# A two-layer block on one core: ascending chunk order, operands of the first heads loaded chunk by chunk, routing moved among the first row maxima

## The chip, the cores and the metric

One core of a Trainium2 chip. Five engines run their own instruction streams side by side: TensorE (PE, with its weight loads as PEld), VectorE (DVE), ScalarE (ACT), GpSimd (POOL) and SyncE (SP), which here only issues DMAs. The metric is the time of one execution on the device in microseconds (us); lower is better.

## The reference

2048 tokens of 256 features go through two gated layers, each `x = x + s * silu(g)` with `xn = layernorm(x)` in front.

```python
# layer 0: s = linear attention by running sums, g = ternary-weight projection
q, k = elu(q) + 1, elu(k) + 1
out = q * cumsum(k * v) / (q * cumsum(k) + 1e-9)
# layer 1: s = causal softmax attention, 16 heads of 16, with a position slope per head
scores = where(causal, q @ k.T / 4 + slope[h] * (k_pos - q_pos), -1e9)
s = softmax(scores) @ v @ out_w.T + out_b
# g = mixture of 8 experts, the best 2 of each token
logits = xn @ gate_w.T + gate_b
routing = softmax(top_k(logits, 2))
for e in range(8):
    h = xn @ w1[e].T + b1[e]
    y = h[:, 0::2] * sigmoid(1.702 * h[:, 0::2]) * (h[:, 1::2] + 1)
    g += (y @ w2[e].T + b2[e]) * routing_weight[:, e]
```

## The kernel before

Layer 0 takes the first 150 us. Then come the projections of layer 1, in four **chunks** of 512 tokens (`c`, `NC = 4`). For each chunk PE makes four 128x512 blocks `m` of q and k. ACT evicts each into `QV` and rounds it to bf16 (`QP[.., 0]`), DVE subtracts (L1032, into `QR`), ACT rounds the rest (L728), DVE subtracts again (L1041); the three bf16 parts go by DMA into the DRAM tensor `qk_parts` (SP, L357). A head's operands in `OPS` are loaded from there by `load(h)`: 6 DMAs of 16 to 48 rows, each over all 2048 columns (L369). On top of them 12 rows with positions and slopes are needed: for heads 0 to 3 ACT writes them (`first_of`, L766), for later heads POOL (`rows`, L527, four instructions for two heads).

Attention runs over 8 **pairs** of heads. A pair has four chunks of queries, taken in `ORDER = (0, 3, 1, 2)`; chunk `a` has 8(a+1) score tiles of up to 128x512, so a pair has 80 tiles and the whole 640. All engines walk through the same numbered **steps** `n`. In step `n`

- PE makes A tile `n` (`score_a`, L1424, masked by L1427) and DVE reduces it to row maxima (`reduce_a`, L1163);
- PE makes B tile `n - 44` (`score_b`, L1444; `LEAD = 44`), the same scores less their row maximum, ACT takes the exponential (L811), and every fourth step PE multiplies four of them with the values (L1466).

Between the two passes, each chunk `m` (numbered through the pairs, four to a pair) needs a **turn**: when its last A tile is reduced, DVE writes `NM` (L1171), POOL splits it in five small instructions into three bf16 parts `NP` (`maxima(m)`, L540 to L548), PE transposes `NP` (`turn_maxima`, L1474) at step `TURN_AT`, ACT copies it to `MT` (L793), and SP writes it by DMA as three more rows of `OPS`, for which the chunk's first B tile waits. `turn_maxima` waits for the five instructions of POOL; everything behind it on PE waits with it.

POOL's order in pair `p` (1 to 6) is fixed in the code:

```python
maxima(NC * p)
maxima(NC * p + 1)
pool.wait_ge(b_scored, PER_PAIR * p)      # the pair before has made its last B tile: step 80p + 43
rows(2 * p + 2); rows(2 * p + 3)          # four instructions of 12x2048
head_values(2 * p + 2); head_values(2 * p + 3)
maxima(NC * p + 2)
maxima(NC * p + 3)
```

The expert layer runs among the same steps. DVE finds the two best experts of each token and each token's place in its expert's list: first some 50 small instructions by themselves (L1081 to L1110), then 15 in steps 3 to 17 (`slots`). ACT and POOL split the normalized tokens in two f16 parts (`XR`, L773 and L560), POOL scatters the rows by 32 indirect DMAs (L569) between `maxima(0)` and `maxima(3)`. 23 blocks of 256 rows follow, block `b` at step `84 + 20b` (24 matmuls of L1361 over eight steps, the 8 of L1371 14 steps later: `down`). In the last pair (`p = 7`) POOL gathers the results by 32 indirect DMAs (L580) between its `maxima`, and DVE adds them up (`add_experts`). Bank 7 is shared by turns, `heads_out` (L1481) and `down`, each of which waits until the one before has been read out.

Of the kernel before, what the change touches and what calls it, by code (L numbers as in the profile page):

```python
# [14 lines left out]
ALU = mybir.AluOpType  # L15
# [3 lines left out]
P = 128  # L19
# [19 lines left out]
ORDER = (0, 3, 1, 2)  # L39
# [12 lines left out]
FIRST_BLOCK, EVERY = 84, 20  # L52
# [30 lines left out]
TURN_AT = {chunk_end(m) - 1 + (3, 4, 5, 3)[m % NC]: m for m in range(NC * PAIRS)}  # L83
HEADS_AT = {chunk_end(m) - 1 + LEAD + (15, 11, 11, 11)[m % NC]: m for m in range(NC * PAIRS)}
# [5 lines left out]
END_PAIRS = [2 * c + r for c in ORDER for r in range(2)]  # L90
END_AT = {650: 0, 655: 1, 661: 2, 665: 3, 675: 4, 679: 5}
# [11 lines left out]
def build(nc, x, w_qkv0, w_out0, w_ffn, b_ffn, w_qkv1, b_qk1, b_v1, w_out1, b_out1, slopes, pos_rows, pick,  # L103
          masks, ident, sel, table, gate_w, gate_b, w1, b1, w2, b2, out):
    ctx = ExitStack()
    with ctx:
# [3 lines left out]
        def sem(name):  # L110
# [39 lines left out]
        TH = sb("TH", [P, 2, CH])  # L150
        GT = sb("GT", [P, 2, CH])
# [32 lines left out]
        XTH, XTL = XT[:, 0], XT[:, 1]  # L184
        WQG = 3 * D + E
# [11 lines left out]
        TAB = pr32[:, S + D:S + D + E * NT + 8 + 24]  # L197
# [27 lines left out]
        QV = ops32[:, 0:2048].rearrange("p (m n) -> p m n", m=4)  # L225
        QR = ops32[:, 2048:4096].rearrange("p (m n) -> p m n", m=4)
        QP = ops32[:, 4096:7168].bitcast(BF16).rearrange("p (m j n) -> p m j n", m=4, j=3)
# [33 lines left out]
        v_copied, lg_copied, gsplit, route = (  # L261
            sem("v_copied"), sem("lg_copied"), sem("gsplit"), sem("route"))
        expd, rstep, ones_rows, we_done, wet_ps = (
            sem("expd"), sem("rstep"), sem("ones_rows"), sem("we_done"), sem("wet_ps"))
# [12 lines left out]
        hot, count_ps, chain, slots_done, xr_high, xr_low = (  # L277
            sem("hot"), sem("count_ps"), sem("chain"), sem("slots_done"), sem("xr_high"), sem("xr_low"))
# [10 lines left out]
        b2_zero, wet_zero = sem("b2_zero"), sem("wet_zero")  # L289
# [31 lines left out]
        def _(sp):  # L321
# [31 lines left out]
            with sp.Fori(0, NC) as c:  # L353
                for m in range(4):
                    side, half = m // 2, m % 2
                    sp.wait_ge(qk_p2, 4 * c + m + 1)
                    sp.dma_start(parts[side, :, half * P:half * P + P, ds(c * CH, CH)].rearrange("j f t -> f j t"),  # L357
                                 QP[:, m, :, :]).then_inc(parts_out[m], 16)

# [1264 lines left out]
```

## Time and profile before

| | |
|---|---|
| time, median of 3 (lowest to highest) | 972.3 us (968.9 to 974.0) |
| the profiled execution's own time | 969.48 us |
| its span | 967.7 us, of mean granted TensorE clock 0.923 |
| PE busy | 796.4 us (82%) |
| DVE busy | 635.3 us (66%) |
| ACT busy | 498.7 us (52%) |
| POOL busy | 313.9 us (32%) |

Busy time is a share of the whole span. A PE that shows busy is not at its peak, since matmuls are pipelined. The row of the page with the span in 40 slices of 24.2 us each shows where PE is not busy: up to slice 5 (layer 0), in slices 8 and 9, and in slice 33:

```
PE   4474659914889999999999999999999995888986
```

### The profile page before, as it was taken

Reading aid. Unit: us, or ns where it says so; the run is one execution under the profiler, and the core shown is the slowest. Engines: PE = TensorE matmul, PEld = TensorE weight load, DVE = VectorE, ACT = ScalarE, POOL = GpSimd, SP = SyncE. Lnnn points to the kernel's source line nnn. Section 1 sums busy time; section 2 is a strip of 40 time slices with the busy share of each in tenths; the row PEclk is TensorE's granted clock in tenths of the full one; section 3 lists DMA queues with packets and bytes.
Section 4 is the critical chain, followed back from the end, with each engine's and each line's share of the span. In section 5 each row is a group of like instructions: output and inputs, shape, how many; then the busy total and the mean of one; then the engine's idle time right before and its main releaser. Section 6 shows DMA issues by size and latency. Waiting matters only on the chain.

```text
span 967.7 us, 13783 instructions
## 1 busy us (share of the span) xinstructions
PE 796.4 (82%) x4910; PEld 387.1 (40%) x4910; DVE 635.3 (66%) x1197; ACT 498.7 (52%) x1030; POOL 313.9 (32%) x363
## 2 busy tenths in 40 slices
PE   4474659914889999999999999999999995888986
PEld 1242345403324444444544444444444432222543
DVE  5999997665856666676566667666666763984121
ACT  2343315861555565555555655555565552556340
POOL 2766963121660060051006005100600516340111
PEclk9797979966799999999999999999999997999795
DMA  9501302332223235225223532522353112111110
GB/s 322 173 0 66 109 22 87 131 108 70 102 93 88 67 99 100 76 63 107 62 66 103 101 73 65 106 62 66 98 108 71 40 49 77 45 55 68 42 34 33
DMA packets 72392, 80.03 MB, mean 83 GB/s; under 512 B 33561, under 2 KB 56020, under 8 KB 72196
## 3 DMA queue, kind: packets, MB, share of 16 engines
q1 hardware_dynamic: 67660, 68.84, 26.0%
q0 software_dynamic: 3296, 8.62, 2.9%
q10 hardware_dynamic: 1368, 1.70, 0.6%
q8 instruction: 39, 0.64, 0.3%
q14 instruction: 29, 0.24, 0.1%
HBM read 34.22 MB, written 26.74 MB: 63 GB/s over the span
## 4 chain that ended last, share of the span: by engine, by line
PE 55%; DVE 26%; issue 7%; POOL 3%; DMA 3%; ACT 3%; SPq 1%; POOLq 0%; ACTq 0%; DVEq 0%
PE bank L1466 14%; DVE PM L1163 11%; PE bank L1424 10%; PE bank L1444 7%; PE bank L1361 5%; PE bank L1371 5%; PE bank L1481 3%; DVE PR L960 3%; PE bank L1256 2%; PE bank L1508 2%; DMA OPS<-qk_parts 2%; DVE YT L1062 2%; POOL XT L580 1%; POOL x_rows L569 1%; PE bank L1427 1%
## 5 line engine op out<-in xcount | busy, mean ns | idle before, releaser
L1163 DVE TENSOR_REDUCE PM<-bank 128x1 f32<-128x512 f32 (+3 forms) x640 | 368.6, 605 | 217.7 <-PE bank L1427 160.1
L811 ACT ACTIVATE PR<-bank 128x512 f32<-128x512 f32 (+3 forms) x640 | 331.6, 536 | 302.7 <-PE bank L1447 150.7
L1424 PE MATMUL bank<-OPS 108*128 108x512 bf16 (+3 forms) x640 | 228.5, 361 | 72.3 <-DVE PM L1163 36.1
L1444 PE MATMUL bank<-OPS 111*128 111x512 bf16 (+3 forms) x640 | 225.0, 354 | 3.3 <-ACT PR L811 3.1
L1466 PE MATMUL bank<-PR,VS 128*17 128x512 f32 (+3 forms) x1280 | 159.0, 548 | 0.5 <-ACT PR L811 0.4
L540 POOL TENSOR_TENSOR NP<-NM,NIL 128x8 bf16<-128x8 f32 x32 | 6.5, 202 | 429.9 <-DVE NM L1171 429.8
L1424 PEld LDWEIGHTS bank<-OPS 108*128 108x128 bf16 x640 | 64.2, 100 | 193.3 <-DVE PM L1163 131.9
L1361 PE MATMUL bank<-WB 128*128 128x256 f16 x552 | 90.7, 272 | 0.0
L527 POOL TENSOR_TENSOR OPS<-POSR,SCL 12x2048 bf16<-12x2048 bf16 x24 | 87.8, 3680 | 7.6 <-PE bank L1447 7.6
L1444 PEld LDWEIGHTS bank<-OPS 111*128 111x128 bf16 x640 | 63.3, 99 | 39.0 <-ACT PR L811 15.6
L1361 PEld LDWEIGHTS bank<-WB 128*128 128x128 f16 x552 | 49.5, 99 | 44.6 <-issue 22.3
L1427 PE MATMUL bank<-MASK 128*128 128x128 bf16 x256 | 57.7, 225 | 0.0
L1447 PE MATMUL bank<-MASK 128*128 128x128 bf16 x256 | 57.4, 225 | 0.0
L1299 PE MATMUL bank<-VV,YT 128*128 128x256 f32 x64 | 21.4, 506 | 36.1 <-DVE YT L964 36.1
L1256 PE MATMUL bank<-XT,VV 128*128 128x512 f16 x144 | 35.2, 407 | 13.1 <-issue 11.6
L1371 PE MATMUL bank<-WB,YT 128*128 128x256 f32 x184 | 45.9, 392 | 0.0
L1481 PEld LDWEIGHTS bank<-SEL,U 128*128 128x128 f32 x256 | 32.1, 197 | 26.3 <-issue 26.3
L1371 PEld LDWEIGHTS bank<-WB,YT 128*128 128x128 f32 x184 | 33.1, 189 | 23.1 <-issue 19.5
L1466 PEld LDWEIGHTS bank<-PR,VS 128*17 128x17 f32 x1280 | 21.3, 96 | 49.2 <-issue 29.0
L580 POOL DMA_INDIRECT XT<-y_rows,SLOT x32 | 30.9, 966 | 18.2 <-DVE ACC L1075 9.8
L1481 PE MATMUL bank<-SEL,U 128*128 128x34 f32 x256 | 35.7, 286 | 0.8 <-ACT U L800 0.8
L569 POOL DMA_INDIRECT x_rows<-XT,SLOT x32 | 31.0, 968 | 14.1 <-issue 9.1
(187 smaller groups left out, 975.8 us busy)
## 6 DMA issues: line engine op xcount, KB each, us to landing
qk_parts<-OPS SPq DMA_DIRECT2D x16, 384.0 KB, 3.6
OPS<-qk_parts SPq DMA_DIRECT2D x32, 192.0 KB
x_rows<-PR SPq DMA_DIRECT2D x23, 256.0 KB, 3.6
WB<-W1H SPq DMA_DIRECT2D x23, 256.0 KB, 2.4
WB<-W1L SPq DMA_DIRECT2D x23, 256.0 KB, 2.4
WB<-in_w SPq DMA_DIRECT2D x23, 256.0 KB, 2.7
y_rows<-XT SPq DMA_DIRECT2D x23, 256.0 KB, 2.2
OPS<-qk_parts SPq DMA_DIRECT2D x32, 128.0 KB
```

Source lines behind the costliest of these rows:

```text
L527: pool.tensor_tensor(OPS[0:POS, h % 4, side, :], POSR[:, side, :], SCL[:, side, h:h + 1].broadcast_to([POS, S]), ALU.mult).then_inc(opa_ro ...
L811: act.activation(PR[:, tile % RING, off:CH], PS[2 + tile % 2][:, off:CH], ACT.Exp).then_inc(b_exped, 1)
L1163: dve.tensor_reduce(PM[:, c % 2, j, xq, gg:gg + 1], bank[:, 0:width], AX.X, ALU.max).then_inc(a_reduced, 1)
L1256: done = mm(out, w if weight_first else d, d if weight_first else w, start=first and k == 0 and j == 0, stop=last and k == KK - 1 and j == 2)
L1361: last = mm(PS[5 + f][:, SLOTS * part:SLOTS * part + SLOTS], W1B[b % 2][:, wp, col:col + P], XB[b % 2][:, dp, k, :], start=j == 0, stop=j ...
L1371: last = mm(PS[7][:, D * q:D * q + D], YT[:, b % 2, f, P * q:P * q + P], W2B[b % 2][:, f, :], start=f == 0, stop=f == KK - 1)
L1424: last = mm(bank[:, 0:width], OPS[0:ROWS_A, h % 4, 0, P * (TC * a + xq):P * (TC * a + xq) + P], OPS[0:ROWS_A, h % 4, 1, CH * gg:CH * gg + ...
L1427: last = mm(bank[:, P * xq:P * xq + P], MASK[:, 0, :], MASK[:, 2, :], start=False, stop=True)
L1444: last = mm(bank[:, off:CH], OPS[0:ROWS_B, h % 4, 1, P * k:P * k + P], OPS[0:ROWS_B, h % 4, 0, CH * b + off:CH * b + CH], start=True, stop ...
L1447: last = mm(bank[:, off:off + P], MASK[:, 1, :], MASK[:, 2, :], start=False, stop=True)
L1466: last = mm(PS[4][32 * n:32 * n + HD + 1, off:CH], VS[:, (2 * p + j) % 4, k, :], PR[:, (first + n) % RING, off:CH], start=b > 0 and k0 == ...
L1481: last = mm(PS[7][:, wide * q:wide * q + wide], U[:, m % 2, P * q:P * q + P], SEL[:, :], start=True, stop=True)
```

## The change

- `ORDER` becomes `(0, 1, 2, 3)`, in every pair. The chunks of a pair now end behind its tiles 8, 24, 48 and 80 (before 8, 40, 56 and 80). The turn comes 5 steps behind a chunk's last A tile (`TURN_AT`, before 3, 4, 5, 3), so at steps 12, 28, 52 and 84 of a pair (before 10, 43, 60 and 82).
- The first two heads are loaded chunk by chunk: SP sends a chunk's four parts out, waits for two of them, and issues 12 DMAs of 512 columns. `QV`, `QR` and `QP` move out of `OPS` into other buffers. The first tile of each chunk waits for that chunk only (`first_in`).
- The 12 extra rows of heads 0 and 1 are written by POOL (`rows(0)`, `rows(1)`), as soon as the slopes are ready, and ahead of the last experts' weights; before, ACT wrote them behind the projections.
- Routing is 36 DVE instructions (`sort`), two in each of steps 1 to 18, in place of some 50 ahead of the steps and 15 among them; four of them work on 1024 elements a partition and a fifth reduces as many.
- Routing rows and start values (`turn_routing`, `output_biases`) come at steps 19 to 41. Blocks start at step 96. The scatters stand 8, 16 and 8 between the maxima (before 10, 12, 10), the gathers 6, 10 and 16 (before 12, 10, 10).

```diff
-ORDER = (0, 3, 1, 2)
+ORDER = (0, 1, 2, 3)
-FIRST_BLOCK, EVERY = 84, 20
+FIRST_BLOCK, EVERY = 96, 20
-TURN_AT = {chunk_end(m) - 1 + (3, 4, 5, 3)[m % NC]: m for m in range(NC * PAIRS)}
-HEADS_AT = {chunk_end(m) - 1 + LEAD + (15, 11, 11, 11)[m % NC]: m for m in range(NC * PAIRS)}
+TURN_AT = {chunk_end(m) - 1 + 5: m for m in range(NC * PAIRS)}
+HEADS_AT = {chunk_end(m) - 1 + LEAD + 11: m for m in range(NC * PAIRS)}
-ADD_AT = {FIRST_BLOCK + EVERY * BLOCKS + 28 + 3 * n: t
+ADD_AT = {FIRST_BLOCK + EVERY * BLOCKS + 20 + 3 * n: t
...
+BIAS_AT = {19 + 2 * k: k for k in range(NC + NT // 2)}
...
-            for m in range(4):
-                sp.wait_ge(parts_out[m], 16 * NC)
-            load(0)
-            load(1)
+            for c in range(NC):
+                cols = slice(CH * c, CH * c + CH)
+                for m in range(4):
+                    side, half = m // 2, m % 2
+                    sp.wait_ge(qk_p2, 4 * c + m + 1)
+                    sp.dma_start(parts[side, :, half * P:half * P + P, cols].rearrange("j f t -> f j t"),
+                                 QP[m]).then_inc(parts_out[m], 16)
+                sp.wait_ge(parts_out[0], 16 * c + 16)
+                sp.wait_ge(parts_out[2], 16 * c + 16)
+                for h in range(2):
...
+                            sp.dma_start(OPS[row:row + rows, h, side, cols], src).then_inc(first_in[c], 16)
...
+            for m in range(4):
+                sp.wait_ge(parts_out[m], 16 * NC)
             load(2)
             load(3)
...
             rstd(2 * NC, ds(TC * (NC - 1), TC))
-            pool.wait_ge(outT, 2 * NC)
-            pool.memset(WET[:, :], 0.0).then_inc(wet_zero, 1)
-            scale(E // 2 - 1)
-            pool.wait_ge(w1l_done, E - 2)
-            low_parts(E // 2 - 1)
...
             pool.wait_ge(scl, 8)
             pool.wait_ge(cast_in, 32)
-            for m in range(4):
-                pool.wait_ge(parts_out[m], 16 * NC)
-            pool.wait_ge(w1l_done, E)
+            rows(0)
+            rows(1)
+            scale(E // 2 - 1)
+            pool.wait_ge(w1l_done, E - 2)
+            low_parts(E // 2 - 1)
...
-            scatter(range(0, 5))
+            scatter(range(0, 4))
             maxima(1)
-            scatter(range(5, 11))
+            scatter(range(4, 12))
             maxima(2)
-            scatter(range(11, NT))
+            scatter(range(12, NT))
...
-                    gather(0, GATHERS)
+                    gather(0, 3)
                 maxima(NC * p)
                 if p == PAIRS - 1:
-                    gather(GATHERS, 11)
+                    gather(3, 8)
                 maxima(NC * p + 1)
                 if p == PAIRS - 1:
-                    gather(11, NT)
+                    gather(8, NT)
...
-                if 3 <= n < 18:
-                    slots(n - 3)
+                if 1 <= n <= SORTED // 2:
+                    sort(2 * n - 2)
+                    sort(2 * n - 1)
```

Three places show how the instructions stand. POOL, at the end of its share in layer 0 and behind it; before:

```order
L460 TENSOR_TENSOR RSTD<-VEPS,HALF 128x4 x2
L519 MEMSET PR 128x2048
L498 TENSOR_SCALAR PR<-PR 128x1024 x2
L505 TENSOR_TENSOR W1L<-PR,W1H 128x1024 x2
L532 COPY VS<-VV 128x16x16 x2
```

and of the change:

```order
L474 TENSOR_TENSOR RSTD<-VEPS,HALF 128x4 x2
L535 TENSOR_TENSOR OPS<-POSR,SCL 12x2048 x4
L512 TENSOR_SCALAR PR<-PR 128x1024 x2
L519 TENSOR_TENSOR W1L<-PR,W1H 128x1024 x2
L540 COPY VS<-VV 128x16x16 x2
```

The four row instructions now stand where the memset stood, ahead of the weights of experts 6 and 7, and reach POOL while DVE is at the subtractions of the first chunks.

DVE, in steps 0 to 4 of the change (L1186 is a tile's row maximum, the others routing; before, nothing of this size stood there, and all routing down to `WTS` stood ahead of step 0):

```order
L1186 TENSOR_REDUCE PM<-bank 128x1 x2
L1108 TENSOR_TENSOR YT<-LG 128x1024
L1110 TENSOR_TENSOR YT<-LG 128x1024
L1186 TENSOR_REDUCE PM<-bank 128x1
L1112 TENSOR_TENSOR YT<-YT,PR 128x1024
L1115 TENSOR_TENSOR YT<-YT 128x1024
L1186 TENSOR_REDUCE PM<-bank 128x1
L1117 TENSOR_REDUCE U<-YT 128x128
L1119 TENSOR_SCALAR U<-U 128x128
```

All 36 routing instructions now stand between the row maxima of the first 19 tiles.

PE, in pair 1 around the turn of the pair's third chunk. L1444 or L1469 is a B tile, L1371 or L1392 `down`, L1466 or L1491 values. Before, at steps 58 to 60 of the pair:

```order
L1466 MATMUL bank<-PR,VS 17x512 x4
L1371 MATMUL bank<-WB,YT 128x256 x4
L1424 MATMUL bank<-OPS 128x512
L1444 MATMUL bank<-OPS 128x512
L1424 MATMUL bank<-OPS 128x512
L1444 MATMUL bank<-OPS 128x512
L1474 MATMUL bank<-MASK,NP 24x128
```

and of the change, at its steps 50 to 52:

```order
L1491 MATMUL bank<-PR,VS 17x384
L1392 MATMUL bank<-WB,YT 128x256 x4
L1449 MATMUL bank<-OPS 128x128
L1452 MATMUL bank<-MASK 128x128
L1469 MATMUL bank<-OPS 128x128
L1472 MATMUL bank<-MASK 128x128
L1449 MATMUL bank<-OPS 128x512
L1469 MATMUL bank<-OPS 128x512
L1499 MATMUL bank<-MASK,NP 24x128
```

The B tile 128 wide is the last of the pair's chunk 0, so the turn comes right behind the first B tile of the next chunk: 9 steps behind the pair before, where it was 17. POOL's rows in pairs 1 to 6 stand as before (two `maxima`, the four of `rows`, two copies, two `maxima`).

## Rows read from the trace of the kernel before

**Rows 1.** Busy time of each engine by stage; the header names the columns.

```profile
core 0: us, PE busy (x) PEld busy (x) DVE busy (x) ACT busy (x) POOL busy (x), PEclk, DMA share, GB/s
147.90:198.70 50.80, 48.23 (x250) 25.32 (x247) 34.92 (x74) 39.49 (x88) 13.14 (x9) 0.97 0.32 109
198.70:230.00 31.30, 0.03 (x1) 0.06 (x2) 14.40 (x45) 11.94 (x13) 10.51 (x12) 0.53 0.32 105
230.00:258.60 28.60, 25.34 (x114) 13.75 (x114) 26.39 (x62) 14.84 (x17) 11.99 (x21) 0.80 0.26 91
258.60:337.90 79.30, 72.49 (x469) 30.86 (x468) 49.90 (x98) 45.21 (x96) 24.96 (x42) 0.96 0.28 84
469.00:553.50 84.50, 78.95 (x551) 38.89 (x550) 55.37 (x109) 49.29 (x109) 19.25 (x26) 1.00 0.35 82
```

**Rows 2.** Timeline, projections to first tile: start us, us, engine line, [idle before <-releaser].

```profile
161.61 2.48 DVE L1041 TENSOR_TENSOR OPS<-OPS 128x512 bf16<-128x512 f32 x4
162.46 37.38 SPq L357 DMA_DIRECT2D qk_parts<-OPS  x16
165.17 0.63 ACT L722 ACTIVATE OPS<-OPS 128x512 bf16<-128x512 f32 x1 [2.61 <-DMA qk_parts<-OPS]
172.64 2.49 DVE L1041 TENSOR_TENSOR OPS<-OPS 128x512 bf16<-128x512 f32 x4
...
203.20 12.05 SPq L369 DMA_DIRECT2D OPS<-qk_parts  x12
229.97 0.27 PE L1424 MATMUL bank<-OPS 108*128 108x128 bf16 x1 [31.92 <-DMA OPS<-qk_parts]
```

**Rows 3.** The same timeline, where instructions of POOL and DVE run at once.

```profile
175.80 4.22 POOL L505 TENSOR_TENSOR W1L<-PR,W1H 128x1024 f16<-128x1024 f32 x2 [17.65 <-ACT W1H L678]
178.18 3.59 DVE L1032 TENSOR_TENSOR OPS<-OPS 128x512 f32<-128x512 f32 x3 [3.05 <-ACT OPS L722]
207.26 0.28 DVE L1097 TENSOR_TENSOR U<-U,LG 128x128 f32<-128x128 f32 x1
211.49 9.02 POOL L560 TENSOR_TENSOR XT<-ACC,XT 128x512 f16<-128x512 f32 x8 [7.30 <-ACT XT L773]
218.37 1.12 DVE L1108 TENSOR_TENSOR U<-U,TOP 128x128 f32<-128x128 f32 x1
```

**Rows 4.** Busy time of L1163 alone in steps 0 to 43: DVE, clock, DMA.

```profile
230.00:258.60 28.60, 24.12 (x44) 0.80 0.26 91
```

**Rows 5.** Timeline of pair 6, POOL and PE, from its step 43 to 60.

```profile
760.63 14.63 POOL L527 TENSOR_TENSOR OPS<-POSR,SCL 12x2048 bf16<-12x2048 bf16 x4 [1.27 <-PE bank L1447]
761.14 0.49 PE L1361 MATMUL bank<-WB 128*128 128x256 f16 x3
770.60 1.08 PE L1481 MATMUL bank<-SEL,U 128*128 128x34 f32 x8
775.21 0.73 POOL L532 COPY VS<-VV 128x256 f32<-128x256 f32 x2
775.78 1.99 PE L1371 MATMUL bank<-WB,YT 128*128 128x256 f32 x8
777.01 0.20 POOL L548 TENSOR_TENSOR NP<-NR,NIL 128x8 bf16<-128x8 f32 x1
779.39 0.23 PE L1474 MATMUL bank<-MASK,NP 128*24 128x128 bf16 x1 [0.74 <-ACT XT L757]
```

**Rows 6.** Timeline of pair 7: first and last of 12 gathers, and PE's turn.

```profile
799.07 1.04 POOL L580 DMA_INDIRECT XT<-y_rows,SLOT  x1 [0.56 <-issue]
813.02 0.96 POOL L580 DMA_INDIRECT XT<-y_rows,SLOT  x1 [0.30 <-issue]
815.47 0.27 PE L1474 MATMUL bank<-MASK,NP 128*24 128x128 bf16 x1 [10.23 <-POOL NP L548]
```

**Rows 7.** By stage, columns as in rows 1: the two stretches behind that wait.

```profile
815.30:818.30 3.00, 2.83 (x11) 1.41 (x12) 1.61 (x4) 1.34 (x3) 0.02 (x1) 0.50 0.03 5
818.30:821.30 3.00, 3.00 (x14) 0.57 (x11) 1.45 (x3) 1.09 (x2) 1.93 (x2) 0.50 0.17 46
```

More of the change, by code:

```diff
@@ L378, in rows_out @@
                         "j (q t) -> j q t", q=TC), MT[3 * TC * j:3 * TC * j + 3 * TC, m % 2, :]).then_inc(mrow[m % NC], 16)
-            for m in range(4):
-                sp.wait_ge(parts_out[m], 16 * NC)
-            load(0)
-            load(1)
+            for c in range(NC):
[8 more added lines that the diff above has]
+                for h in range(2):
+                    for side in range(2):
+                        row = POS
+                        for first, parts_of, times_of in LOADS[side]:
+                            rows = HD * parts_of * times_of
+                            src = parts[side, first:first + parts_of, HD * h:HD * h + HD, cols]
+                            if times_of > 1:
+                                src = src.broadcast_to([times_of, HD, CH])
+                            sp.dma_start(OPS[row:row + rows, h, side, cols], src).then_inc(first_in[c], 16)
+                            row += rows
             sp.wait_ge(memset_done, 11)
@@ L721, in _ @@
                     wait(act, parts_out[m], 16 * c)
-                    act.activation(QP[:, m, 0, :], QV[:, m, :], ACT.Copy).then_inc(qk_p0, 1)
+                    if c == 0 and m == 2:
+                        act.wait_ge(x1_add, 2 * NC)
+                    act.activation(QP[m][:, 0, :], QV[:, m, :], ACT.Copy).then_inc(qk_p0, 1)
                 if c + 1 < NC:
@@ L727, in _ @@
                     wait(act, qk_r1, 4 * c + m + 1)
[L728 removed]
+                    act.activation(QP[m][:, 1, :], QR[:, m, :], ACT.Copy).then_inc(qk_p1, 1)
                 values(c, (2, 3))
@@ L1117, in slots @@
-            def slots(k):
-                if k == 0:
-                    dve.wait_ge(count_ps, 1)
-                    dve.wait_ge(table_in, 16)
-                    dve.wait_ge(we_done, 2)
-                else:
-                    dve.wait_ge(chain, k)
-                if k == 0:
+            over = TMP.rearrange("p t e -> p (t e)")[:, 0:8 * E].rearrange("p (e j) -> p e j", e=E)
+            own = LG[:, :, :].unsqueeze(3).broadcast_to([P, NT, E, E])
+            other = LG[:, :, :].unsqueeze(2).broadcast_to([P, NT, E, E])
@@ L1412, in score_a @@
                 width = CH if gg < a else P * (xq + 1)
+                if p == 0 and tile == OFF[c]:
+                    pe.wait_ge(first_in[c], 16 * 12)
                 if tile % PER_PAIR == 0:
-                    pe.wait_ge(opa_in[p % 2], 16 * 12 * (p // 2 + 1))
-                    if p >= 2:
-                        pe.wait_ge(opa_rows, 4 * p - 4)
+                    wait(pe, opa_in[p % 2], 16 * 12 * ((p + 1) // 2))
+                    if p == 1:
+                        pe.wait_ge(first_rows, 4)
                     else:
-                        pe.wait_ge(first_rows, 4 * p + 4)
+                        pe.wait_ge(opa_rows, max(4, 4 * p))
                 if tile < WIDE:
@@ L1512, in _ @@
             pe.wait_ge(cast_in, 32)
-            side_work = [(turn_routing, c) for c in range(NC)] + [(output_biases, r) for r in range(NT // 2)]
             for n in range(STEPS):
@@ L1516, in _ @@
                     score_a(n)
-                    if n % 2 and n // 2 < len(side_work):
-                        stage, which = side_work[n // 2]
-                        stage(which)
-                if n == 1:
+                    if n in BIAS_AT:
+                        if BIAS_AT[n] < NC:
+                            turn_routing(BIAS_AT[n])
+                        else:
+                            output_biases(BIAS_AT[n] - NC)
+                if n == 5:
                     count_tokens()
```

220 lines of the change are left out of this document (114 added, 106 removed).

## The prediction

> **What bounds the kernel now.** I read the busy time by stage first, then the timeline at each place where PE is not busy. [Rows 1] show three different stretches. In a pair in the middle (469.0 to 553.5) PE is busy 78.95 of 84.50 us at full clock, DVE 55.37, ACT 49.29: PE sets the pace, at 84.5/80 = 1.06 us a step, and any wait of PE is added to the time. Five pairs read the same. From 198.7 to 230.0 PE does nothing: in [rows 2] it waits 31.92 us for the operand loads, which SP could only issue from 203.20 on. From 230.0 to 258.6 (steps 0 to 43, A tiles alone) DVE is busy 26.39 of 28.60 us: DVE sets the pace. A fourth place is in pair 7: PE waits 10.23 us at a turn, behind 12 gathers on POOL [rows 6].
>
> So the change aims at two waits that exist, 31.3 us and 10.2 us. What else it moves has to be priced on the engine that sets the pace at that place.
>
> **The projections: +12 us.** POOL now runs the four row instructions from the moment the slopes are ready. They are 3.66 us each (14.63 for four, [rows 5]) and would run from about 161.5 to 176. DVE begins the subtractions of chunk 0 at 161.61, four in 2.48 us [rows 2]; both operands lie in SBUF. [Rows 3] show what such an instruction does beside POOL: three subtractions took 3.59 us instead of about 2, as POOL ran L505; an instruction that takes 0.28 us alone took 1.12 us while POOL ran instructions of 9.02/8 = 1.13 us, and ended at 219.49, just behind the seventh of them (211.49 + 7 x 1.13 = 219.4). So DVE gets about one in per POOL instruction. Four subtractions behind four instructions of 3.66 us end near 161.5 + 4 x (3.66 + 0.62) = 178.6, where before they ended at 164.1: 14.5 us late. Chunk 1's ACT rounding waits for chunk 0's parts in DRAM (2.61 us in [rows 2], the wait is there already), so the delay is handed on; some slack of DVE between chunks (34.92 busy in 50.80, [rows 1]) takes back 2 to 3. I take 12. Bounds: 3 if DVE is not held up at all (the experts' weights on POOL come 3 us later than ACT wants them), 15 if nothing is taken back.
>
> The Trainium skill, page "SBUF — State Buffer", section "SBUF: two separate sides", says that DVE with two SBUF inputs and a GpSimd instruction that reads SBUF take an exclusive lock, and the later one "fully blocks". By that rule the delay would be the 12 to 15 above, and without the rule 3; the trace's 1.12 against 0.28 us agrees with the rule.
>
> SP's chunk loads are hidden: 12 DMAs of full length took 12.05 us to issue [rows 2], so at most that per chunk, plus 2.7 for stores and 2.6 to land, 17 against a chunk's period of 11 to 13. At 12.05 SP would fall some 4 us behind a chunk; with a quarter of the bytes each I take 8 to 9. Chunk 3 is needed only at step 48, and has 20 us and more to spare either way.
>
> **The gap: -31.3 us.** Tiles start when PE ends the projections, at 198.7 + 12 = 210.7.
>
> **Steps 0 to 43: +19 us.** 44 row maxima took 24.12 us of DVE [rows 4]. With ascending chunks the first 44 tiles have 18,048 columns instead of 18,816, so 23.2. Routing: five instructions on 1024 elements, by the 0.62 us for 512 some 1.2 each, 6.1; 31 small ones at the 0.28 of [rows 3], 8.7. Sum 38.0, plus 2 for PE's own starts and waits. The eight instructions of POOL on `XT` [rows 3] now run beside the first eight routing instructions, each of which waits up to 1.13: +7. That is 47, against 28.6 before: +18.4, bounds +11 (no such waits) and +24. The 14.4 us of routing that lay under the gap have lost their cover.
>
> Step 44 so comes at 258, where it was 258.6. **The start gains nothing: -0.6 us**, bounds -19 to +8. The stretch to step 124, 79.30 us [rows 1], I leave as it is; POOL scatters 16 x 1.26 = 20 us between two maxima, about what the steps between them take.
>
> **The turn of the third chunk, pairs 1 to 6: +61 us.** In the trace POOL's `rows` start at 760.63, at the pair's step 43, and end 14.6 us later, the copies at 775.9, and the five small ones of `maxima` at 777.2 [rows 5]. PE asks for them at 779.39, 17 steps behind step 43: 2.2 us to spare. In the change PE asks at step 52, 9 steps behind. `maxima(4p+2)` still stands behind `rows` on POOL. PE's own 18.9 us for the 17 steps hold eight triples of L1361 (0.33 each by their starts, 2.6), `down` 1.99 and L1481 1.08 [rows 5]; the rest, 13.3/17 = 0.78 us a step. Nine steps with `down` (now at step 50): 7.0 + 2.0 = 9.0 us. POOL needs 777.21 + 0.2 - 760.63 = 16.8 us. **PE waits 7.8 us.** All that is queued behind the turn on PE waits too, and DVE and ACT run dry.
>
> After the 10.23 us wait PE ran at clock 0.50, the level of 1.2 GHz, for 6 us while busy 5.83 [rows 7]: 2.9 us lost. For 7.8 us I take 2.4. Together 10.2 a pair, six pairs: 61 us. Bounds: 7.0 (a pace of 1.0 a step leaves a wait of 5.8, and 1.2 lost to the clock) and 12.5 (a pace of 0.7, a wait of 8.5, and 4 lost to clock and refilling), so 42 to 75. Nothing gives it back, since PE has only 5.6 us of idle time in a pair.
>
> **The gathers: -9 us.** Six gathers ahead of `maxima(28)` instead of 12 take 6 x 1.26 (by the starts 799.07 to 813.02 in [rows 6], 13.95/11 = 1.27) = 7.6 us, and its turn comes two steps later. POOL would be ready at 799.07 + 7.6 + 1.4 = 808.1 by the times of before, PE at 805.2 + 1.7 = 806.9: a wait of 1 us. So 10.2 + 2.9 - 1 = 12 come back. The other 26 gathers stand before the next two turns: 12.6 us for 16 steps and 20.2 us for 24 leave one or two us late each; I deduct 3.
>
> **Small ones: +3 us.** A turn now stands two steps behind a `down` twice in a pair (steps 10 and 12, 50 and 52; before once), and waits for its bank as in [rows 5] (0.74): 8 x 0.3 to 0.7. The last 44 B tiles are wider by four diagonal ones, under 1 us.
>
> **Sum** against the profiled execution: 969.5 - 0.6 + 61 - 9 + 3 = 1024 us. The execution lies 0.3% below the median of 972.3, too little to shift it. A measurement of this kernel tells about 0.5% (5 us) from no change.
>
> **The rivals.**
>
> *The start gains.* The same six waits, but DVE is held up less: the first row instructions slip between, or POOL gets behind DVE instead. For it: in [rows 3] the three subtractions beside L505 lost 1.5 us together, no more than one wait, so a row of subtractions may not wait each time. Against it: the 1.12 us. With bounds 3 and +11 the start gains 17, and the time is 1007. Chance 0.14.
>
> *The waits in the pairs don't appear* (the other side). If PE reached step 52 only 16.8 us behind step 43, POOL would be ready. That needs 1.65 us a step besides `down`, more than twice the 0.78 of the rows; it would hold if DVE's gate instructions of a block, which read two SBUF operands, were held up by `rows` for whole instructions and PE behind them. But a block's up matmuls lie in that stretch of the trace too, so such waits are inside the 18.9 already. Then the time is 969.5 - 0.6 - 9 + 3 = 963, and 946 with the start's gain. It decides in favour of faster once the wait is under 1 us a pair. Chance 0.05.
>
> *More comes late behind each wait.* SP's rows of `MT` stand behind 12 operand loads (12 us from step 43) and a block's fetch behind these; the B tiles of step 68 wait for them. By the rows SP is done near 21 us behind step 43, PE arrives after 31: 10 us to spare. If that were eaten, or the clock stayed low until the next wait, a pair would cost 14, and the time 1047. Chance 0.09.
>
> *No visible change*: the gains of the start and the gathers just cover six smaller waits. Chance 0.02. That leaves 0.70 for the forecast, whose own range is 1010 to 1038.
>
> **How the numbers follow.** The forecast's range and the first rival hold 0.84; from 998 to 1040 is the range for 8 in 10, its upper end at a wait of 12.5 a pair. Slower holds 0.70 + 0.14 + 0.09 = 0.93, no change 0.02, faster 0.05.
>
> **What would show it.** In the trace of the change: PE's turn L1499 with an idle time of 7 to 9 us, released by POOL, six times, 90 to 95 us apart; a granted clock of 0.50 behind each; a pair of about 95 us by windows; the subtractions L1057 of chunk 0 ending near 178; the first A tile near 211 and the first B tile near 258; a turn in the last pair that waits under 2 us. The prediction is wrong if the first A tile comes before 204, or if L1499 shows no long wait from POOL.

## The result and the profile after

The changed kernel takes 1022.6 us (median of 4 runs, 1021.2 to 1024.1); the kernel before, on the same chip, took 972.8. The ratio is 1.052, with a 95% interval of 1.049 to 1.055. Ratios compare fast executions only; one slow execution, 1085 us of the kernel before with its gathers spread, is left out of its ratio. The profiled execution spans 1019.4 us against 967.7: 51.7 us more.

First the granted clock and the busy time in the page's 40 slices.

```profile
PE   4574578747999699969996998799789969889896
PEclk9787888776699989989997999799989989999995
```

The PEclk row dips once about every four slices: a low clock comes back once in each pair. The stages by windows, as in [rows 1]:

```profile
core 0: us, PE busy (x) PEld busy (x) DVE busy (x) ACT busy (x) POOL busy (x), PEclk, DMA share, GB/s
147.90:213.50 65.60, 54.64 (x253) 27.65 (x252) 48.08 (x74) 39.55 (x89) 28.62 (x13) 0.84 0.30 97
213.50:268.00 54.50, 35.02 (x120) 15.74 (x121) 40.91 (x83) 19.37 (x27) 39.65 (x46) 0.59 0.36 124
268.00:341.20 73.20, 68.87 (x461) 29.15 (x460) 48.80 (x96) 44.05 (x94) 11.69 (x30) 0.98 0.22 64
485.40:581.00 95.60, 82.30 (x550) 40.28 (x550) 54.97 (x108) 49.66 (x108) 19.07 (x26) 0.95 0.29 73
246.00:249.00 3.00, 2.40 (x10) 1.44 (x11) 2.60 (x6) 1.04 (x3) 2.50 (x7) 1.00 0.32 117
255.00:258.00 3.00, 3.00 (x8) 1.44 (x7) 1.29 (x2) 0.53 (x2) 2.29 (x3) 0.50 0.37 133
549.70:557.70 8.00, 7.99 (x32) 4.00 (x33) 3.26 (x7) 3.02 (x6) 0.00 (x0) 0.50 0.35 118
```

The first row is the projections' end, 65.6 us where [rows 1] have 50.8. The gap of 31.3 us is gone. The second row is steps 0 to 43: 54.5 us for 28.6. The fourth is a pair: 95.6 for 84.5, with PE busy 82.3 for 78.95 (the same instructions at a lower clock) and idle 13.3 us for 5.55. The two rows of 3 us lie ahead of the first B tile and are taken up below. The last row stands right behind a turn in that pair: PE is busy throughout, at the lower of its two clock levels. The timeline of POOL and PE in that pair, as in [rows 5]:

```profile
533.17 14.44 POOL L535 TENSOR_TENSOR OPS<-POSR,SCL 12x2048 bf16<-12x2048 bf16 x4 [18.98 <-PE bank L1472]
547.57 0.73 POOL L540 COPY VS<-VV 128x256 f32<-128x256 f32 x2
549.37 0.20 POOL L556 TENSOR_TENSOR NP<-NR,NIL 128x8 bf16<-128x8 f32 x1
549.71 0.26 PE L1499 MATMUL bank<-MASK,NP 128*24 128x128 bf16 x1 [6.62 <-POOL NP L556]
```

PE came at 543.09, 9.9 us behind step 43, and POOL was ready 16.4 us behind it. The wait of 6.62 us stands in each of the six pairs. The row instructions of the six pairs start at 341.20, 437.31, 533.17, 628.89, 724.53 and 820.15. In the kernel before the first of them starts at 338.13 and the sixth at 760.63 [rows 5]. So the first comes 3.1 us later; five pairs of 84.5 us became 478.95 us, 56.4 more; from the sixth to the end there are 199.2 us where there were 207.1, 7.8 less. Together 51.7.

The projections and the start, by the timeline, as in [rows 2, 3] (the L1057 row is the end of chunk 0's second subtractions, the two L1048 rows behind it are chunk 1's first):

```profile
161.67 17.87 POOL L535 TENSOR_TENSOR OPS<-POSR,SCL 12x2048 bf16<-12x2048 bf16 x4 [7.28 <-DVE B1S L1040]
162.79 1.28 DVE L1057 TENSOR_TENSOR TG<-YT,TG 128x512 bf16<-128x512 f32 x2
166.30 5.78 DVE L1048 TENSOR_TENSOR YT<-PR,WB 128x512 f32<-128x512 f32 x2 [2.23 <-ACT WB L734]
172.00 8.09 DVE L1048 TENSOR_TENSOR YT<-PR,TG 128x512 f32<-128x512 f32 x2
188.05 1.28 DVE L1057 TENSOR_TENSOR TG<-YT,TG 128x512 bf16<-128x512 f32 x2
190.91 0.69 DVE L1048 TENSOR_TENSOR YT<-PR,WB 128x512 f32<-128x512 f32 x1 [1.58 <-ACT WB L734]
213.50 0.22 PE L1449 MATMUL bank<-OPS 108*128 108x128 bf16 x1 [0.59 <-issue]
214.17 12.85 POOL L570 TENSOR_TENSOR XT<-ACC,XT 128x512 f16<-128x512 f32 x8
214.35 2.05 DVE L1108 TENSOR_TENSOR YT<-LG 128x1024 f32<-128x1024 f32 x1
227.32 0.29 PE L1402 MATMUL bank<-HOT,MASK 128*128 128x128 bf16 x1 [12.49 <-DVE HOT L1123]
240.95 1.01 PE L1414 MATMUL bank<-IDN,WE 128*8 128x128 f32 x4 [2.32 <-DVE WE L1175]
258.64 2.07 PE L1425 MATMUL bank<-PR 8*128 8x256 f32 x4
268.05 0.63 PE L1469 MATMUL bank<-OPS 111*128 111x512 bf16 x1
880.48 0.22 PE L1499 MATMUL bank<-MASK,NP 128*24 128x128 bf16 x1 [0.95 <-POOL NP L556]
```

Two engines hold each other up. Four subtractions of DVE, each 0.69 us when it runs apart from POOL, took 13.8 us from first to last, and four instructions of POOL that take 14.44 us took 17.87. It was chunk 1's subtractions that were caught; chunk 0's, from 161.59 to 164.1, got by, and it was POOL's first row instruction that took 5.86 us instead of 3.59. The last row is the turn in the last pair that used to wait 10.23 us [rows 6].

### The profile page after: what moved, and what is told of

It reads as the page before. It is cut to its first block, busy times and chain, and to the rows that moved or that the text cites. A ratio compares the mean times of both kernels' runs of the same rounds, so it can differ in the third digit from the quotient of the medians.

```text
span 1019.4 us, 13738 instructions
## 1 busy us (share of the span) xinstructions
PE 823.8 (81%) x4910; PEld 397.2 (39%) x4910; DVE 646.0 (63%) x1173; ACT 493.1 (48%) x1026; POOL 334.2 (33%) x365
## 4 chain that ended last, share of the span: by engine, by line
PE 54%; DVE 22%; POOL 12%; issue 6%; ACT 4%; DMA 1%; POOLq 0%; ACTq 0%; DVEq 0%
PE bank L1491 13%; PE bank L1449 10%; POOL OPS L535 9%; PE bank L1469 8%; DVE PM L1186 6%; PE bank L1382 6%; PE bank L1506 4%; PE bank L1392 3%; DVE PR L976 3%; PE bank L1532 2%; DVE ACC L881 2%; PE bank L1280 2%; PE bank L1425 1%; ACT PR L820 1%; DVE OPS L953 1%
## 5 line engine op out<-in xcount | busy, mean ns | idle before, releaser
L1186 DVE TENSOR_REDUCE PM<-bank 128x1 f32<-128x512 f32 (+3 forms) x640 | 370.3, 606 | 273.3 <-PE bank L1452 161.4
L1449 PE MATMUL bank<-OPS 108*128 108x512 bf16 (+3 forms) x640 | 236.0, 373 | 47.9 <-DVE PM L1186 45.3
L1469 PE MATMUL bank<-OPS 111*128 111x512 bf16 (+3 forms) x640 | 229.8, 361 | 6.5 <-ACT PR L820 6.2
L1491 PE MATMUL bank<-PR,VS 128*17 128x512 f32 (+3 forms) x1280 | 156.9, 541 | 1.2 <-ACT PR L820 0.4
L535 POOL TENSOR_TENSOR OPS<-POSR,SCL 12x2048 bf16<-12x2048 bf16 x28 | 104.5, 3757 | 121.2 <-PE bank L1472 113.9
L1382 PE MATMUL bank<-WB 128*128 128x256 f16 x552 | 93.6, 279 | 0.0
L1469 PEld LDWEIGHTS bank<-OPS 111*128 111x128 bf16 x640 | 64.0, 100 | 49.4 <-ACT PR L820 23.1
L1472 PE MATMUL bank<-MASK 128*128 128x128 bf16 x256 | 56.4, 220 | 0.0
L1323 PE MATMUL bank<-VV,YT 128*128 128x256 f32 x64 | 23.8, 551 | 34.7 <-DVE YT L980 34.7
L1280 PE MATMUL bank<-XT,VV 128*128 128x512 f16 x144 | 36.0, 414 | 13.3 <-DVE XT L889 12.4
L1506 PEld LDWEIGHTS bank<-SEL,U 128*128 128x128 f32 x256 | 35.9, 217 | 27.1 <-issue 26.6
L1392 PE MATMUL bank<-WB,YT 128*128 128x256 f32 x184 | 45.9, 392 | 0.0
L1499 PE MATMUL bank<-MASK,NP 128*24 128x128 bf16 x32 | 7.5, 234 | 43.3 <-POOL NP L556 41.1
L1491 PEld LDWEIGHTS bank<-PR,VS 128*17 128x17 f32 x1280 | 21.3, 96 | 52.0 <-issue 27.3
L1392 PEld LDWEIGHTS bank<-WB,YT 128*128 128x128 f32 x184 | 33.1, 189 | 20.5 <-issue 16.9
L1506 PE MATMUL bank<-SEL,U 128*128 128x34 f32 x256 | 39.6, 304 | 0.8 <-ACT U L809 0.8
```

The costliest lines, as they stand in the source:

```text
L535: pool.tensor_tensor(OPS[0:POS, h % 4, side, :], POSR[:, side, :], SCL[:, side, h:h + 1].broadcast_to([POS, S]), ALU.mult).then_inc(opa_ro ...
L1186: dve.tensor_reduce(PM[:, c % 2, j, xq, gg:gg + 1], bank[:, 0:width], AX.X, ALU.max).then_inc(a_reduced, 1)
L1280: done = mm(out, w if weight_first else d, d if weight_first else w, start=first and k == 0 and j == 0, stop=last and k == KK - 1 and j == 2)
L1382: last = mm(PS[5 + f][:, SLOTS * part:SLOTS * part + SLOTS], W1B[b % 2][:, wp, col:col + P], XB[b % 2][:, dp, k, :], start=j == 0, stop=j ...
L1392: last = mm(PS[7][:, D * q:D * q + D], YT[:, b % 2, f, P * q:P * q + P], W2B[b % 2][:, f, :], start=f == 0, stop=f == KK - 1)
L1449: last = mm(bank[:, 0:width], OPS[0:ROWS_A, h % 4, 0, P * (TC * a + xq):P * (TC * a + xq) + P], OPS[0:ROWS_A, h % 4, 1, CH * gg:CH * gg + ...
```

## The experiments

**The order on POOL.** The theory to test is that six waits behind the row instructions make the loss. One kernel moves all four behind `maxima`, one moves two, and one leaves POOL alone and lets PE come later.

```diff
+                maxima(NC * p + 2)
                 if 1 <= p < PAIRS - 1:
                     pool.wait_ge(b_scored, PER_PAIR * p)
                     rows(2 * p + 2)
                     rows(2 * p + 3)
...
-                maxima(NC * p + 2)
                 maxima(NC * p + 3)
```

> The changed kernel with one thing turned round: on POOL the five small instructions of the third chunk's `maxima` stand ahead of the four row instructions of the next pair, not behind them. Theory (the row instructions ahead of the maxima make the six waits, with the slow clock behind each; together 11.1 us a pair): PE's turn waits under 1 us for POOL, a pair takes 84.5 to 85.5 us, and the time falls by 6 x 11.1 = 67 us, to 951 to 960. Rival A (the ascending order of the chunks itself costs, by narrow tiles in another sequence or by what DVE and ACT do): a pair stays above 90 and the time above 985. Rival B (the row instructions, now 5 to 10 us later, make something else late: the first tiles of the next pair or the fourth chunk's turn): the wait at the third turn is gone, another of 3 us or more a pair stands elsewhere, and the time is 965 to 985.

Measured: 968.7 us, 0.997 of the kernel before (0.994 to 1.000). So 54 us came back, where the theory had 67. The longest wait for POOL at a turn is 1.0 us, and it is none of the six. By the starts of the row instructions (347.13 and, the sixth, 782.01) a pair takes 87.0 us, not 84.5. One place of rival B is in the chain of waits; the rows are what PE waits for, in total, times, longest:

```profile
PE bank L1469 <- DMA OPS<-MT: 8.0, 6, 2.1
PE bank L1499 <- POOL NP L556: 1.0, 1, 1.0
```

The rows of `MT` are late now (8.0 us in all): with the turn's wait gone, SP's DMAs, which the prediction had named as late next, come last at these places. That is 1.3 of the 2.5 us of a pair; rival B is right in kind and small in size.

```diff
                 if 1 <= p < PAIRS - 1:
                     pool.wait_ge(b_scored, PER_PAIR * p)
                     rows(2 * p + 2)
+                maxima(NC * p + 2)
+                if 1 <= p < PAIRS - 1:
                     rows(2 * p + 3)
...
-                maxima(NC * p + 2)
```

> The changed kernel with the row instructions of one head (two of the four, 7.2 us) moved behind the third chunk's `maxima`, the other two still ahead. A dose between the changed kernel and the one with all four behind. Theory (the wait is what POOL's queue ahead of the maxima lasts, less what PE needs to its turn): POOL is ready 7.2 us (and the 1.5 us of the head's copies, which also stand behind now) earlier than the 6.6 us by which it was late, so the wait is under 0.5 us and the time 951 to 962, as with all four behind. Rival (any row instruction that runs in these steps slows DVE and PE, wait or not): the time lies half way, 980 to 995.

Measured: 970.9 us, 1.000 of the kernel before (0.997 to 1.003). None of the six waits is left, as with all four moved, so the wait is the queue's length less PE's way to the turn, and the rival with half the loss falls. But this is 9 us above the theory's upper end, and again it is the pair. Windows of two pairs, from row instructions to row instructions:

```profile
518.67:604.97 86.30, 78.86 (x552) 38.85 (x550) 54.75 (x109) 49.23 (x109) 19.06 (x27) 1.00 0.34 81
604.97:692.40 87.43, 80.33 (x552) 39.64 (x550) 54.63 (x109) 49.23 (x109) 19.05 (x26) 0.98 0.34 79
```

Five pairs from 345.43 to 779.20 give 86.75 us each. The first window has PE at full clock and as busy as in [rows 1] (78.86 for 78.95), and is idle 7.44 us for 5.55. Its waits for row maxima are 5.1 us in 8 times, where a pair before had 4.4 in 10, and 0.7 is for `MT`. The second window has no turn waiting for POOL either, but PE busy 80.33 us at a mean clock of 0.98: a short stretch at the low clock comes back.

```profile
608.00:612.00 4.00, 2.42 (x21) 0.91 (x18) 3.81 (x7) 1.92 (x5) 4.00 (x2) 0.96 0.30 89
612.00:616.00 4.00, 4.00 (x17) 2.69 (x14) 0.00 (x0) 0.00 (x0) 3.69 (x7) 0.61 0.19 71
```

Of the ten pairs of this trace and the one with all four moved, six have full clock and take 85.6 to 86.8 us, and four have the low stretch and take 87.4 to 88.5. So the ascending order costs about 2.25 us a pair on average without any turn waiting, 1.1 to 2.3 at full clock and 3 to 4 with the low stretch, and the wait proper costs 95.6 - 86.75 = 8.85. Which part of the order leaves PE that idle time was not tried apart.

```diff
-TURN_AT = {chunk_end(m) - 1 + 5: m for m in range(NC * PAIRS)}
+TURN_AT = {chunk_end(m) - 1 + (9 if m % NC == 2 and m > NC else 5): m for m in range(NC * PAIRS)}
```

> The changed kernel with PE's turn of the third chunk four steps later in every pair from the second on (step 56 of a pair, not 52); POOL's queue is untouched. Theory: PE arrives 4 x 0.8 = 3.2 us later, so the six waits shrink from 6.6 to about 3.4 us. If the other 4.5 us of a pair's 11.1 (slow clock, emptied buffers) come with each wait whatever its length, a pair costs 8 us more than before and the time is 1001; if they shrink with it, 5.7 us and 988. Rival (the wait is not POOL's doing but the order's): no change, 1018 to 1024.

Measured: 985.4 us, 1.014 (1.009 to 1.020), near the branch in which the rest shrinks with the wait. Two of the six turns:

```profile
448.45 0.27 PE L1499 MATMUL bank<-MASK,NP 128*24 128x128 bf16 x1 [2.93 <-POOL NP L556]
628.51 0.22 PE L1499 MATMUL bank<-MASK,NP 128*24 128x128 bf16 x1 [1.35 <-POOL NP L556]
```

Four steps were worth 5.3 us, not 3.2, so that five waits are 1.3 to 1.4 us and one 2.93. The last pairs take 88.73 us (611.97 to 700.70), with PE busy 80.57. Over the mean of 86.75 of a pair without a wait that is 2.0 us for 1.35 of wait, against 8.85 for 6.62. But pairs without any wait for POOL take up to 88.5 when the low clock comes, so what a short wait costs on top of itself can't be read from this; that the loss as a whole shrinks with the wait can.

**The gathers alone, in the kernel before.**

```diff
-                    gather(0, GATHERS)
+                    gather(0, 3)
...
-                    gather(GATHERS, 11)
+                    gather(3, 11)
```

> The kernel before with one part of the change alone: the gathers of the last pair spread. Three token tiles' gathers ahead of the first `maxima` of the last pair, not six, and the next eight ahead of the second (there the order of the chunks forbids the 3, 5 and 8 of the change, since the sums that free the gather buffers come in between), five ahead of the third as before. Theory of the prediction: the wait of 10.2 us before the first turn falls to 1 to 3 us and the slow clock behind it goes, so 9 to 13 us come back, and 3 may be lost at the second turn, behind 16 gathers (20 us) where 10 stood: 960 to 965. Rival (PE had slack behind that wait, in the end of the last pair, so that the wait is made good): 970 to 973, no change.

Measured: 961.3 us, 0.990 (0.986 to 0.994) of the kernel before, 9.9 us less; in the spans 967.7 to 959.2, 8.5. The turn's wait fell from 10.23 to 2.68:

```profile
809.66 0.22 PE L1474 MATMUL bank<-MASK,NP 128*24 128x128 bf16 x1 [2.68 <-POOL NP L548]
```

So this part of the change pays by itself.

**The row instructions in the projections.** They go to ACT, ahead of a wait that ACT has there anyway.

```diff
+                    if c in (1, 2) and m == 0:
...
+                        first_of(c - 1)
                     wait(act, parts_out[m], 16 * c)
...
-            rows(0)
-            rows(1)
             scale(E // 2 - 1)
```

> The changed kernel with its first four row instructions (two heads) taken from POOL and given to ACT, which writes them in the projections' second and third chunk, ahead of its wait for the parts' DMA (1.99 us each on ACT in this trace, in idle stretches of 2.4 and 5.4 us). Everything else, the six waits too, stays. Theory (POOL's row instructions hold up DVE's subtractions, which put the end of the projections 12 to 15 us back): the pairs of subtractions of chunk 1 take 1.3 us again and not 5.8 and 8.1, the first A tile comes near 200 to 203 and not at 213.5, and the time falls by 10 to 13 us, to 1009 to 1013. Rival (the projections are late by the chunk loads that share DMA queues and SP with the parts' stores, or by the experts' weights behind POOL): the subtractions take less but the first A tile stays beyond 209, and the time beyond 1017.

This kernel, the next one and the first two with the old order (further down) were measured side by side at a time when the kernel before too took 986.9 us, some 15 more than otherwise, so their ratios are not set beside the others'. This one took 1045.7, 1.057 (1.050 to 1.063), and whether the time fell can't be told from it. Its timeline in the projections is free of what made these runs long:

```profile
167.08 0.69 DVE L1051 TENSOR_TENSOR YT<-PR,WB 128x512 f32<-128x512 f32 x1 [3.60 <-ACT WB L743]
184.07 0.69 DVE L1051 TENSOR_TENSOR YT<-PR,WB 128x512 f32<-128x512 f32 x1 [7.70 <-ACT WB L743]
162.63 3.90 ACT L722 ACTIVATE OPS<-POSR,SCL 12x2048 bf16<-12x2048 bf16 x2
206.73 0.22 PE L1452 MATMUL bank<-OPS 108*128 108x128 bf16 x1 [0.59 <-issue]
```

All of chunk 1's subtractions take 0.69 us again. The first A tile comes at 206.7, 6.8 us sooner and not 10 to 13, since ACT's 7.8 us were only partly in idle time: DVE now waits 3.6 and 7.7 us for ACT at the heads of chunks 1 and 2. So the hold-up between POOL and DVE is shown, and the mending costs about half of what it mends. What is left of the 6.8 us further on can't be read here; the kernel with both mendings, below, shows it.

**POOL's subtractions beside the routing.** Moved behind the first `maxima` and the wait for the slots:

```diff
             maxima(0)
             pool.wait_ge(sorting, PLACED)
+            for r in range(NT // 2):
+                pool.wait_ge(xr_high, r + 1)
+                pool.tensor_tensor(XR[:, 2 * r:2 * r + 2, 1, :], XN[:, 2 * r:2 * r + 2, :],
...
```

> The changed kernel with POOL's eight subtractions on the tokens' low parts (12.85 us beside the routing's first instructions) moved behind the first `maxima` and the wait for the slots, so that they run when the routing has ended; the 32 scatters start some 9 us later. Theory (the two engines hold each other up): the routing's five instructions on 1024 elements take 1.2 us each and not 1.7 to 2.06, the expert count on PE comes 3 to 5 us earlier, but from there PE at its slow clock sets the pace beside the output biases, so the first B tile comes only 3 to 4 us earlier (264 to 265 where it was 268.05) and the time falls by 3, to 1017 to 1021. Rival (the later scatters hold the second turn): the first B tile comes later than 268 or a wait for POOL of more than 5 us appears before 290, and the time is 1024 to 1035.

Measured, beside the last one: 1056.2 us, 1.068 (1.060 to 1.076). Rows of DVE and PE:

```profile
214.88 1.28 DVE L1108 TENSOR_TENSOR YT<-LG 128x1024 f32<-128x1024 f32 x1
220.87 1.21 DVE L1117 TENSOR_REDUCE U<-YT 128x128 f32<-128x1024 f32 x1
223.15 0.29 PE L1402 MATMUL bank<-HOT,MASK 128*128 128x128 bf16 x1 [7.78 <-DVE HOT L1123]
253.08 0.27 PE L1499 MATMUL bank<-MASK,NP 128*24 128x128 bf16 x1 [5.46 <-POOL NR L554]
```

The five large routing instructions take 6.2 us together (9.1 in the changed kernel), and the count comes 9.1 us behind the first A tile, not 13.8: the theory's 3 to 5 us. They are lost at the next turn, which waits 5.46 us for POOL, as the rival has it. So it is no mending. Its first B tile, at 278.19, has a standstill of the kind described below just ahead of it, and the changed kernel wasn't measured beside it, so the time says nothing more.

**What sets the pace in steps 24 to 43.** The output biases' matmuls on 32 of 256 columns; this leaves out seven eighths of the output biases.

```diff
-                    last = mm(PS[4 + r % 2][:, D * q:D * q + D], WET[0:E, P * tile:P * tile + P], B2[0:E, :],
+                    last = mm(PS[4 + r % 2][:, D * q:D * q + 32], WET[0:E, P * tile:P * tile + P], B2[0:E, 0:32],
```

> The changed kernel with the output biases' 16 matmuls on 32 of 256 columns; it leaves out seven eighths of the output biases (the other columns start from what lies in the bank). In the changed kernel these 32 instructions take about 16.6 us of PE in the 19 us before the first B tile, at a granted clock of 0.50, where PE is busy 3.00 of every 3.00 us. Theory (there PE at its slow clock, with the biases among the A tiles, sets the pace, not DVE as the prediction had it): DVE's idle time of 1.8 us ahead of each pair of row maxima goes, and the first B tile comes 8 to 12 us sooner (256 to 260 in a trace where it was 268), the whole time falls by as much. Rival (DVE or ACT's copies set the pace): the first B tile moves by less than 3 us.

> The changed kernel itself, unchanged, beside the kernel before on the same chip as the two others of this call, as their reference. 1.049 to 1.055 times the kernel before, as measured first.

Measured side by side: the changed kernel again 1025.4 us, 1.056 (1.050 to 1.062), as before; with narrow biases 1017.5, 1.047 (1.041 to 1.054). The first B tile comes at 262.50, and at 267.43 in this second trace of the changed kernel: 4.9 us, between theory (8 to 12) and rival (under 3). The same window as above says why it is not more:

```profile
255.00:258.00 3.00, 3.00 (x12) 1.52 (x11) 1.65 (x5) 1.19 (x2) 2.34 (x3) 0.50 0.37 135
```

PE has 12 instructions in 3 us where it had 8, and is still busy 3.00 at clock 0.50. DVE is busy 1.65 of 3.00, so it isn't the bound. PE at the lower of its levels (1.2 GHz) sets the pace. An eighth of the columns doesn't take an eighth of the time: four of the narrow matmuls take 1.06 us at this clock, where four whole ones take 2.07. All 32 took 14.3 us in the changed kernel (the expectation had 16.6) and 7.5 here. In the kernel before four whole ones took half as long, at full clock:

```profile
240.93 1.08 PE L1404 MATMUL bank<-PR 128*128 128x256 f32 x4
```

**The change without its reordering**, with POOL's row instructions and with ACT's. The chunks' order, the turns' steps, the first block's step and the split of the scatters are those of the kernel before; the gathers are 3, 8 and 5 token tiles.

```diff
-ORDER = (0, 1, 2, 3)
+ORDER = (0, 3, 1, 2)
...
-FIRST_BLOCK, EVERY = 96, 20
+FIRST_BLOCK, EVERY = 84, 20
...
-                if p == 0 and tile == OFF[c]:
-                    pe.wait_ge(first_in[c], 16 * 12)
+                if p == 0 and tile == OFF[c] and c < 2:
+                    for b in range(NC) if c else [0]:
+                        pe.wait_ge(first_in[b], 16 * 12)
```

> The change without its reordering: chunk loads in the projections, routing among the row maxima and spread gathers stay, the chunks' order is 0, 3, 1, 2 again with the turns' and blocks' steps of the kernel before (the gathers are 3, 8, 5 tiles; POOL's first row instructions stay in the projections). Step 8 now needs all four chunks loaded. Theory: the pairs take 84.5 us again and no turn waits for the row instructions; the first A tile comes at 213 as in the changed kernel, then the wait for the last chunk's loads ends near 226, and the 36 tiles and what is left of the routing bring the first B tile to 265 to 270, against 259 before: 7 to 9 us lost there, 9 won in the end of the last pair, so 965 to 972. Rival (the order is innocent of the longer pair, the turn's place alone makes it): the same result; what tells here is whether a pair takes 84.5 us and not 86.5, which is what it took in the ascending order without a wait.

> The same as the kernel with order 0, 3, 1, 2 and chunk loads, and the first four row instructions on ACT in the projections, not on POOL. Theory: 12 us less in the projections, so the first B tile near 253 to 258 and 953 to 960 in all, faster than both kernels. Rival (the row instructions' delay is hidden by another wait, for the chunk loads): no better than with the rows on POOL, 965 to 972.

Measured, both at the time of the long runs: 1004.8 us, 1.018 (1.010 to 1.026), and 993.6, 1.006 (1.002 to 1.010). Both are above what was expected; the pair is 84.5 us in both (369.57 to 454.06 and 356.61 to 441.12). Their traces show stretches in which PE, DVE and ACT stand still together, released by nothing of this core ("remote"), as here in the first of them:

```profile
312.94 1.08 ACT L820 ACTIVATE PR<-bank 128x512 f32<-128x512 f32 x2 [4.56 <-remote]
312.90 0.69 DVE L1186 TENSOR_REDUCE PM<-bank 128x1 f32<-128x512 f32 x1 [6.53 <-remote]
```

So the second of the two ran again later, unchanged:

> The kernel with order 0, 3, 1, 2, chunk loads in the projections and the first row instructions on ACT a second time, since all four kernels of its first call, the kernel before too, showed stretches of 2 to 6 us between 236 and 315 us in which PE, DVE and ACT stood still together, or were some 15 us longer than in the other calls. Without such stretches: pairs of 84.5 us, first B tile 260 to 264, the end of the last pair 9 us shorter than before: 958 to 966, or 0.99 to 0.996 of the kernel before. If it is again over 1.00, the stretches belong to the kernel, not to the call.

Measured: 961.4 us (956.1 to 966.0), 0.988 (0.985 to 0.992), and none of those stretches. They belonged to that time, not to the kernel. The row instructions of the pairs start at 339.51, 424.03, ..., 762.12: 84.5 us a pair. The first B tile comes at 263.94, 5 us later than in the kernel before.

**Both mendings in the ascending order**: two row instructions behind `maxima`, and the first four on ACT.

> The changed kernel with both mendings: two of each pair's four row instructions behind the third chunk's maxima, and the first four row instructions on ACT in the projections. Theory (the two costs lie in different stretches and add): the first alone gave 1.000 times the kernel before; the second brought the first A tile 6.8 us sooner. Together 0.992 to 0.995, 962 to 965. Rival (what the second wins is lost again before the first B tile, as PE at its slow clock sets the pace there): 0.998 to 1.002.

Measured: 963.6 us, 0.992 (0.989 to 0.995), against 1.056 for the changed kernel beside it. The first A tile comes at 205.11, the first B tile at 261.93, both sooner than in the changed kernel (213.63 and 267.43). The two costs add, and the rival falls.

Three kernels are some 1% faster than the kernel before, each with an interval that ends below 1: the kernel before with its gathers spread (0.990), the mended change (0.992), and the change without the reordering, with its first rows on ACT (0.988). They can't be told apart, and the first differs from the kernel before by two numbers only.

## Why the prediction was right, and where its sum was off

**The turn of the third chunk** carried the forecast, and it is what happened: six waits released by POOL, a low clock behind each, a pair of 95.6 us for "about 95". Moving the row instructions away, or the turn, takes the loss away. Of the term's parts, "PE waits 7.8 us" measured 6.6, since PE came 9.9 us behind step 43 and not 9.0, and POOL was ready after 16.4 and not 16.8. "2.4" for the clock was too little: behind each turn PE ran 8 us at 0.50, and was busy 82.3 us in a pair where it is 78.9 at full clock, so 3.4. Against the mean pair of the ascending order without the wait, which has some low clock of its own (PE busy 79.4), the wait and what follows it cost 8.85: 2.9 more busy and 6.0 more idle. Not in the sum was the order's own price: nothing was charged for it in a pair, and it is 2.25 us on average. So the 10.2 of a pair became 11.1: 8.85 and 2.25. The range's bounds, 42 to 75 us for six, hold 67.

**The projections**, "+12": +14.8, by the mechanism named: one subtraction of DVE to each row instruction of POOL. The place was another. Chunk 0's four subtractions were meant to be the ones held up, and ended at 164.1 as before; chunk 1's were, 13.8 us for four. The rival "the start gains" asked for DVE to be held up less. In the kernel with the rows on ACT it wasn't held up at all, and the first A tile still came at 206.7, 8 us behind the 198.7 at which PE ended the projections before; but there ACT had 7.8 us of row instructions instead, so where the start stands with neither is not shown. By the Trainium skill, page "SBUF — State Buffer", section "SBUF: two separate sides", the later of the two "fully blocks"; the trace agrees, with both engines as losers in turn (0.69 us became up to 4.08 us on DVE, 14.44 became 17.87 on POOL).

**Steps 0 to 43**, "47 us": 54.5. This is the step that failed. It took DVE for the bound, because DVE was busy 26.39 of 28.60 us. The same row of [rows 1] has PE busy 25.34 at a clock of 0.80. In the change the turns of routing leave PE idle early on, the mean clock of the stage is 0.59, and the same work takes PE 35.0 us: 25.34 x 0.80 / 0.59 = 34.4. From 240.95 on PE has the routing rows and the biases beside its A tiles. Its clock is up from about 244 to 250, then PE, busy 2.40 of 3.00 us just before, falls back to 0.50 and stays there, busy 3.00 of every 3.00, until 267, a microsecond ahead of the first B tile. DVE waits 12.6 us for it. DVE's own work was not underrated: it was busy 40.91 us where the sum had 45. The routing up to 240.95 took 27.4 us, 4.7 of them by POOL's subtractions beside it, where "+7" was charged. Of "the start gains nothing: -0.6" became 9.4 us lost at the first B tile.

**The stretch behind it**, left at 79.3 us, took 73.2, and so the start as a whole lost 3.1. It was not tried apart, but the traces account for the 6 us: PE waits 3.8 us less for POOL behind scatters, and one of two `down`s (8 matmuls, 2.0 us) has moved out of the stretch, since the first block comes 12 steps later. The second of these is work put off, not saved.

**The gathers**, "-9": in the kernel before, alone, -8.5 by the spans, and the turn's wait of "1 us" measured 0.95 in the change. The end of the changed kernel gained more: from the sixth row instructions on 7.8 us less, with the sixth wait's 11 in it, so about 19. Some 10 are the gathers' share (196.9 us for 207.1 from there to the end with the gathers alone). In the ascending order without the wait that stretch is 193.3 us, and it still holds the pair's 2.25; so about 6 us more come with the order. Together that is 16 of the 19; the rest, and which part of the order gives the 6, stay open.

**The small ones**, "+3" for waits on the bank: PE's turns wait 2.1 us for ACT in the whole trace, where before it was 4.4. Nothing was to be charged.

The misses were +10 at the first B tile, +6 in the pairs, -6 in the stretch left alone, and -13 in the end with the small ones. They cancel. The turn of the third chunk was foreseen in kind and size; that the sum, 1024, comes within 2 us of 1022.6 is luck.

## What to carry to other kernels

When work is moved in time, look at what stands ahead of the consumer in its producer's queue: here 5 small instructions behind 14.4 us of row instructions turned 2 us to spare into 6.6 us of waiting, six times, and one swap of lines took the waits away. Before calling one engine the bound of a stage, read the others' busy time together with the clock: an engine that is nearly full at 0.80 of its clock (25.34 of 28.60 us) becomes the bound as soon as idle time brings the clock down. And run the parts alone: of this change the gathers by themselves gave as much as any combination tried.

## What was not expected of the hardware

- POOL and DVE slow each other in both directions: POOL's four row instructions took 17.87 us beside DVE's subtractions and 14.44 elsewhere, its eight subtractions 12.85 beside the routing and 9.18 without; DVE's instruction on 1024 elements took 2.05 and 1.28.
- PE was busy 16.64 of the last 17.00 us ahead of the first B tile (251 to 268), all at a granted clock of 0.50, with small fp32 matmuls of 8 rows with A tiles in between; behind a turn's wait of 6.6 us it was back at full clock in about 8.
- At one time the kernel before took 15 us more than otherwise. The four kernels traced then have stretches of up to 7 us, most of them between 236 and 315 us, in which PE, DVE and ACT stood still together with no releaser on the core. What holds them is not settled.
